# Turning the quantised x2 by DMA instead of by PE and VectorE

## The reference, cut to what matters

```
x = x + tanh(g_xattn) * attention(layernorm(x), ctx)      # 16 heads, int8-like quantised wq and wo
x = x + tanh(g_ffn)   * ffn(layernorm(x))

ffn(x): qx = fp8 values of x / scale, one scale per row
        g, u = qx @ qw_gate.T, qx @ qw_up.T, scaled       # 512 -> 1408
        t = silu(g) * u;  qt = fp8 values of t, one scale per row
        y = qt @ qw_down.T, scaled                        # 1408 -> 512
```

## Time and profile before

| | |
|---|---|
| median of 3 runs | 593.86 us (591.64, 595.87, 593.86) |
| span of the profiled execution, first to last instruction | 589.9 us |
| PE busy | 515.7 us (87%) |
| DVE busy | 516.0 us (87%) |
| ACT busy | 471.3 us (80%) |
| POOL busy | 227.2 us (39%) |
| one steady step, from x_in load to x_in load | 59.2 us |
| DMA, mean over the span | 49 GB/s |

### The profile page before, as it was taken

How to read it: one execution, slowest core, us unless ns; L and a number is a source line. 1 busy time by engine, 2 the same in 40 slices (tenths; PEclk the granted TensorE clock), 3 DMA queues, 4 the chain that set the end, 5 groups by cost and what they waited for, 6 DMA issues and landing times.

```text
span 589.9 us, 10832 instructions
## 1 busy us (share of the span) xinstructions
PE 515.7 (87%) x3456; PEld 326.7 (55%) x3456; DVE 516.0 (87%) x1294; ACT 471.3 (80%) x1148; POOL 227.2 (39%) x212
## 2 busy tenths in 40 slices
PE   0778689999999999999999999999999997965843
PEld 0665466567656765676567656765676554532311
DVE  4999989989799979997999799979997996599794
ACT  4499989999898989898989898989898987783251
POOL 4315134004632463246424642464245422452420
PEclk9899989999999999999999999999999998797888
DMA  8913233011002100210021001100100000000000
GB/s 265 386 62 98 99 108 104 6 54 38 1 2 84 44 0 2 79 47 3 1 74 54 1 1 59 68 2 2 54 37 1 1 2 37 0 2 0 36 1 36
DMA packets 14024, 28.75 MB, mean 49 GB/s; under 512 B 2576, under 2 KB 4624, under 8 KB 13968
## 3 DMA queue, kind: packets, MB, share of 16 engines
q1 hardware_dynamic: 9216, 16.65, 8.0%
q0 software_dynamic: 3328, 11.41, 5.7%
q10 hardware_dynamic: 1424, 0.01, 0.1%
HBM read 23.87 MB, written 4.19 MB: 48 GB/s over the span
## 4 chain that ended last, share of the span: by engine, by line
PE 52%; DVE 26%; issue 10%; ACT 2%; DVEq 0%; POOL 0%; POOLq 0%; ACTq 0%
PE bank_s L808 8%; PE bank_t L873 7%; PE bank_u L828 5%; PE bank_g L828 5%; PE bank_a L815 4%; PE bank_g L815 4%; DVE prob L1305 4%; PE bank_o L915 3%; DVE q L1200 3%; DVE t_sb L1195 2%; DVE t_sb L1239 2%; PE bank_a L839 2%; DVE ts L1490 2%; DVE v_sb L1229 1%; PE bank_g L1049 1%
## 5 line engine op out<-in xcount | busy, mean ns | idle before, releaser
L613 ACT ACTIVATE prob<-prob,neg_max 128x256 f32<-128x256 f32 x256 | 127.4, 505 | 2.5 <-DVE neg_max L1305 2.5
L1305 DVE CUSTOM_DVE_ANT_0 prob<-bank_s,mask_sb 128x256 f32<-128x256 f32 x256 | 96.3, 419 | 13.3 <-PE bank_t L873 5.0
L624 ACT ACTIVATE probT<-bank_t 128x512 f32<-128x512 f32 x128 | 74.0, 590 | 20.5 <-PE bank_t L873 17.2
L398 POOL TENSOR_TENSOR up<-up,wgu_scale 128x512 f32<-128x512 f32 (+1 forms) x42 | 54.9, 1306 | 89.1 <-ACT up L593 89.1
L873 PE MATMUL bank_t<-ident,prob 128*128 128x128 f32 x512 | 78.5, 281 | 3.6 <-ACT prob L613 2.4
L873 PEld LDWEIGHTS bank_t<-ident,prob 128*128 128x128 f32 x512 | 59.1, 143 | 30.3 <-issue 18.4
L808 PE MATMUL bank_s<-kf,qf 32*128 32x256 f32 x512 | 73.1, 403 | 1.9 <-DVE neg_max L1305 1.9
L808 PEld LDWEIGHTS bank_s<-kf,qf 32*128 32x128 f32 x512 | 44.0, 185 | 26.1 <-issue 19.6
L413 POOL TENSOR_TENSOR x<-x,y 128x512 f32<-128x512 f32 x14 | 19.6, 1400 | 96.9 <-DVE y L1503 96.9
L408 POOL TENSOR_TENSOR up<-gate,up 128x512 f32<-128x512 f32 (+1 forms) x42 | 54.4, 1296 | 4.2 <-DVE gate L1365 1.5
L613 ACT ACTIVATION_READ_ACCUMULATOR prob<-prob,neg_max 128x1 f32 x256 | 50.4, 197 | 0.0
(11 more groups left out here) (264 smaller groups left out, 1200.7 us busy)
## 6 DMA issues: line engine op xcount, KB each, us to landing
x_in<-in_x_dram SPq DMA_DIRECT2D x8, 512.0 KB
c_in<-in_ctx_dram SPq DMA_DIRECT2D x8, 512.0 KB
out_dram<-x POOLq DMA_DIRECT2D x7, 512.0 KB, 3.2
mask_sb<-in_mask_BxSxS_ff_dram SPq DMA_DIRECT2D x8, 256.0 KB, 3.7
t_sb<-in_L_ffn_w_down_dram SPq DMA_DIRECT2D x2, 704.0 KB, 5.5
t_sb<-in_L_ffn_w_down_dram POOLq DMA_DIRECT2D x2, 704.0 KB, 5.8
kf<-in_L_xattn_wq_dram SPq DMA_DIRECT2D x1, 1024.0 KB, 11.0
probT<-in_L_xattn_wk_dram SPq DMA_DIRECT2D x1, 1024.0 KB, 13.0
```

The lines of the kernel that those rows point to most:

```text
L398: pool.tensor_tensor(up[:, c % 2, 0:w], up[:, c % 2, 0:w], wu_scale[:, off:off + w], ALU.mult).then_inc(f["u_scaled"], 1)
L613: ins = act.activation(prob[:, head_par, t, :], prob[:, head_par, t, :], ACT.Exp, bias=neg_max[:, head_par, t:t + 1], scale=-1.0, accum_ou ...
L624: act.activation(probT[:, (slot + 3) % 4, :, :].rearrange("p a b -> p (a b)"), T_BANK[(slot + 1) % 2][:, :], ACT.Copy).then_inc(s["turned_ ...
L1305: ins = dve.tensor_tensor_reduce(prob[:, hp, t, :], S_BANK[hp][:, t * L:(t + 1) * L], mask_sb[:, hb, t, :], -1.0, 3.4e38, ALU.add, ALU.min ...
```

## The change

The eight PE transposes of `x2T_turn` and DVE's `x2T_copy` leave the orders of the steady steps and of the tail's batch k. In their place SP issues two DMA transposes per batch, each of one block t (128 x 512 bf16, 128 KB) from xq to its half of x2T. Each adds 16 to `x2T_ready`, so PE waits for 32 per batch. SP guards them: earlier products must have read x2T (`u_ps`, `g_ps`), and `q8_ready` must have reached block t. In a step they stand between the x_in load and the c_in load. Batch e of the tail keeps PE's transposes and DVE's copy.

```diff
@@ -291,14 +291,13 @@
             load8("q", wq)
 
             def step(b, par, A):
-                if not A:
-                    return
-
                 if not first_step(b):
                     need_alone(sp, (s["wq_loaded"], 16), (s["x_plus_ready"], b), (s["x_centred"], b))
                 else:
                     load8("k", wk)
                 sp.dma_start(x_in[:, :, :], x[bass.ds(b, 1)].rearrange("o (t p) c -> p (o t) c", p=P)).then_inc(s["x_loaded"], 16)
+                if b > 2:
+                    turn_x2(b - 1)
                 if not first_step(b):
                     need_alone(sp, (s["wq_loaded"], 16), (s["v_ps"], 2 * b))
                 sp.dma_start(c_in[:, :, :], ctx_in[bass.ds(b, 1)].rearrange("o (t p) c -> p (o t) c", p=P)).then_inc(s["ctx_loaded"], 16)
@@ -311,10 +310,21 @@
 
                 need_alone(sp, (s["wq_loaded"], 16), (s["masked"], 16 * (b - 1)))
                 sp.dma_start(mask_sb[:, par, :, :], mask[bass.ds(b, 1)].rearrange("o (t p) l -> p (o t) l", p=P)).then_inc(s[f"mask_loaded_{par}"], 16)
+            def turn_x2(b):
+
+                B2 = b - 2
+                for t in range(NT):
+                    need(sp, s["u_ps"], 1 + 6 * B2 if B2 else 0)
+                    need(sp, s["g_ps"], 6 * B2)
+                    sp.wait_ge(s["q8_ready"], JOBS * B2 + t + 1)
+                    sp.dma_start_transpose(x2T[:, :, t * P:(t + 1) * P], xq[:, t, :]).then_inc(s["x2T_ready"], 16)
+
             step(0, 0, True)
             step(1, 1, True)
             for b in range(2, NB):
                 step(b, b % 2, True)
+            for b in range(NB - 1, NB + 1):
+                turn_x2(b)
 
             sp.wait_ge(s["stored"], 16 * NB)
 
@@ -1022,7 +1032,7 @@
                 def up_project(slot):
                     c6 = slot - 5
                     if c6 == 0:
-                        pe.wait_ge(f["x2T_ready"], d - 1)
+                        pe.wait_ge(f["x2T_ready"], 32 * (d - 1) if f is s else 1)
                     pe.wait_ge(f["u_ready"], 1 + 6 * B2 + c6)
                     project_ffn(U_BANK, wuT, c6).then_inc(f["u_ps"], 1)
 
@@ -1086,7 +1096,7 @@
                 k.head_turn(0); k.ctxT_turn(0); k.oqT_turn(0); k.head_score(1); k.y_project(0); k.head_turn(1)
                 k.head_turn(2); k.ctxT_turn(1); k.group_pv(1); k.k_project_even(2); k.head_score(3); k.head_turn(3)
                 k.k_project_odd(2); k.head_turn(4); k.k_project_even(3); k.xT_turn(4); k.group_pv(5)
-                k.k_project_odd(3); k.xT_turn(5); k.head_turn(5); k.head_score(5); k.x2T_turn(5); k.sx_turn(6)
+                k.k_project_odd(3); k.xT_turn(5); k.head_turn(5); k.head_score(5); k.sx_turn(6)
                 k.head_turn(6); k.up_project(5); k.gate_project(5); k.q_project_0(6); k.up_project(6)
                 k.gate_project(6); k.head_turn(7); k.up_project(7); k.head_score(7); k.gate_project(7); k.head_turn(8)
                 k.up_project(8); k.q_project_1(7); k.gate_project(8); k.up_project(9); k.head_score(9); k.head_turn(9)
@@ -1099,7 +1109,7 @@
             def tail_order(k, e):
                 k.head_turn(0); k.oqT_turn(0); k.head_score(1); k.head_turn(1); k.group_pv(1); k.head_turn(2)
                 k.y_project(0); k.head_turn(3); k.head_score(3); k.head_turn(4); k.group_pv(5); k.head_turn(5)
-                k.head_turn(6); k.head_score(5); k.head_score(7); k.x2T_turn(5); k.head_turn(7); k.up_project(5)
+                k.head_turn(6); k.head_score(5); k.head_score(7); k.head_turn(7); k.up_project(5)
                 k.gate_project(5); k.up_project(6); k.head_turn(8); k.gate_project(6); k.up_project(7); k.group_pv(9)
                 k.head_turn(9); k.gate_project(7); k.head_turn(10); k.head_score(9); k.up_project(8)
                 k.gate_project(8); k.up_project(9); k.head_turn(11); k.head_turn(12); k.gate_project(9)
@@ -1534,7 +1544,7 @@
             def steady_step_order(k):
                 k.head_mask(0); k.head_mask(1); k.oqT_low(0); k.x_stats(0); k.y_scale(1); k.head_mask(2)
                 k.head_mask(3); k.x_scales(2); k.x2_stats(2); k.x2_centre(3); k.head_mask(4); k.x2_max(3)
-                k.head_mask(5); k.xT_low(5); k.x2_sum_0(4); k.x2_sub_0(4); k.x2_sum_1(4); k.x2_sub_1(4); k.x2T_copy(5)
+                k.head_mask(5); k.xT_low(5); k.x2_sum_0(4); k.x2_sub_0(4); k.x2_sum_1(4); k.x2_sub_1(4)
                 k.head_mask(6); k.sx_copy(7); k.head_mask(7); k.gate_scale(6); k.q_scale_0(7); k.gate_scale(7)
                 k.t_mul(7); k.head_mask(8); k.t_mul(8); k.gate_scale(8); k.head_mask(9); k.q_scale_1(8); k.t_mul(9)
                 k.gate_scale(9); k.t_scales(9); k.gate_scale(10); k.t_mul(10); k.head_mask(10); k.t_sum_0(10)
@@ -1547,7 +1557,7 @@
             def tail_order(k, e):
                 k.head_mask(0); k.head_mask(1); k.oqT_low(0); k.head_mask(2); k.head_mask(3); k.y_scale(1)
                 k.head_mask(4); k.head_mask(5); k.x2_stats(2); k.x2_centre(3); k.x2_max(3); k.head_mask(6)
-                k.head_mask(7); k.x2_sum_0(4); k.x2_sub_0(4); k.x2_sum_1(4); k.x2_sub_1(4); k.x2T_copy(5)
+                k.head_mask(7); k.x2_sum_0(4); k.x2_sub_0(4); k.x2_sum_1(4); k.x2_sub_1(4)
                 k.head_mask(8); k.gate_scale(6); k.head_mask(9); k.gate_scale(7); k.t_mul(7); k.t_mul(8)
                 k.gate_scale(8); k.head_mask(10); k.head_mask(11); k.gate_scale(9); k.t_mul(9); k.t_scales(9)
                 k.gate_scale(10); k.t_mul(10); k.o_norm(14); k.o_norm(15); k.gate_scale(11); k.o_max(15); k.o_max(14)
```

## The result

The changed kernel takes 602.4 us (median of 4 runs, 600.5 to 605.5) against 593.5 us before (4 runs): 8.9 us more, ratio 1.014, 95% interval 1.011 to 1.018. The profiled execution took 603.2 us with a span of 601.3, 11.4 us over the span of before. This one time also shows what lies around a span: 1.9 us. By that measure the 589.9 us of before belong to its fastest run, 591.64 us, and the 601.3 us to a run slightly above the median; so the profiles differ by more (11.4 us) than the medians (8.9 us).

A forecast was written before the change was run, and what follows sets the result against it. PE's order was taken as the path around the x2 turn. Six steps of 3.4 - 1.70 (10.2 us) plus 1.6 in the tail gave 11.8 us, on 593.86: 606 us, forecast range 600 to 614, wider range 595 to 630.

The forecast's parts named there:

- L: Time from the second q8_ready to the x2T_ready count of 32, ahead of the first up projection; taken as 3.4 us.
- the free 1.70 us: Time the DMA has after the second q8_ready in a step before PE would start later than today.
- The formula: Cost per batch at the first up projection is L - 1.70 us; 10.2 us for six steps.
- my lower bound of 2.2 from a plain copy: Low end for L: a plain copy of 128 KB, from the 512 KB store's 3.2 us less 0.96.
- 1.83 free: In the tail, from the second xq's end to the up projection: 1.83 us free, so 1.6 us of cost.
- a step of 60.9 us: Sign in the profile after: distance between x_in loads about 60.9 us against 59.2.
- 2 to 2.5 us of idle PE: Sign: PE idle ahead of the first up projection, released by a DMA into x2T, in each of seven places.
- rival A: Turned write costs nothing over a plain copy: L = 2.2, 3.4 us, 597 us (594 to 600), chance 0.25.
- The mask load: Nearest row for sizing L: 256 KB, queued right behind another transfer on SP, 3.7 us.
- rival C: PE's stall also lowers the clock, 1.7 us each, seven times: 618 us (614 to 630), chance 0.15.
- At most 0.40 to 0.55 us to gain: Largest gain per batch around the x2 turn: 0.55 us on PE, 0.40 us if DVE then holds.
- SP: SP's queue between the x_in and c_in loads: waits at q8_ready cost nothing, c_in about 33 us after x_in.

The follow-up runs named there:

- shadow: Kernel before, with PE's turn and DVE's copy kept, plus the same 14 DMA transposes from SP into space nobody reads: 593.8 us.
- split: Changed kernel with a semaphore per block of x2T, PE waiting for block 1 only ahead of the fourth up projection: 595.1 us.
- q first: Changed kernel with q_project_0 ahead of the first up projection on PE in the steady steps: 603.1 us.
- the third transpose: Changed kernel with an extra transpose of block 1 into unused space ahead of the second, PE waiting for all three: 615.4 us.
- tail by PE: Changed kernel with DMA transposes in the steps only; the tail's batch k is turned by PE and copied by DVE: 599.5 us.
- no turn: Only the first batch's x2 is turned and reused by the other six batches, PE waiting for their own xq alone: 595.0 us, repeated 594.6 us.

## Why the prediction was right, and where it was not

**The step's cost, L minus the free 1.70 us:** shown. The formula gave 0.82 from the measured L; the steps have 0.81. With the same transposes and no wait the cost is gone (shadow), with the wait moved nearly all of it is (split).

**The size of L:** the mis-sized term. I took 3.4 us, near the mask load; it is 2.5, close to my lower bound of 2.2 from a plain copy, so the term was 11.8 us and should have been 6 x 0.82 + 1.1 = 6.0 (the tail had L = 2.96 and 1.83 free). The consequences that I had named were too large with it: a step of 60.9 us (59.98 measured) and 2 to 2.5 us of idle PE (0.8 in five steps, 1.8 in one, 2.6 in the tail). With the measured L my own sum gives 593.86 + 6.0 = 600 us, the upper edge of rival A: a turned write at about the price of a plain copy was nearer to the truth than the forecast's L, and 2.52 lies only just above the 2.5 below which I had called the forecast wrong. The mask load was a poor neighbour: its 3.7 us begin while 512 KB ahead of it are still moving. The two transposes hardly touch, as their issues are 1.3 us apart and each moves for some 0.6 us.

**The rest, 2.9 of the 8.9 us:** two things that the sum left out. In the profile, whose difference is 11.4 us, they are the late landing (1.0 us more wait in one step of six), the clock behind it (1.7 us), and 3.2 us in the tail beyond its own wait. The clock is rival C, which I had counted as an alternative with its own 0.15; it came together with the short L, and in one of the six steps, not in each. I had no term for the late landing. How much of the tail's 3.2 us the transpose in it causes is not shown: with PE's turn back in the tail, 2.7 us of extra tail stayed in that profile. That the forecast of 606 was near 602.4 therefore owes something to luck: 5.8 us too much for L stand against 2.9 us that were missing.

**At most 0.40 to 0.55 us to gain:** wrong, 0.13. I looked at who would hold the path at its end (DVE, 0.40 idle at 341) and not at who is next at its start (ACT's exp, needed by head_turn(6)). A chain that names PE without a gap does not say how much later the next producer would have been.

**SP:** right. The c_in load goes out 33.9 us after x_in (33.1 before), late by nothing but the step's own growth of 0.8 us (usual step).

**What a transpose takes.** The Trainium skill's page "VectorE: DVE Perf Modes" ("The three transpose paths") gave 1309 ns per 128x128 block, 5.2 us for four in a row by my estimate; the transpose of four blocks landed in 2.5. The Trainium skill's page "Advanced Engine Details and Errata" ("X-Bar Transpose (TRN2)") has transposes as fast as regular DMAs. In bytes per second it is not so here: the view of the DMA engines, in 40 slices of 0.1 us from 329 us, shows two bursts of about 220 GB/s, while x_in moved at 377. (x_in comes from DRAM; no run has a plain copy inside SBUF.) For the time this mattered little: 128 KB take 0.60 us at 220 GB/s and 0.35 us at 377, so by this estimate 0.25 of the 2.5 us.

```profile
GB/s 20 20 41 20 0 0 0 0 0 0 0 0 74 212 225 220 212 215 123 29 0 0 0 0 0 41 184 225 223 220 207 166 42 3 0 0 0 0 0 0
```

**The late landing.** The two landings of one step took 4.0 us in the mean and 4.4 at most. It is no accident of one run: with q first they took 4.1 and 4.6 us in the same step, with the third transpose up to 3.6, while the other six kernels with transposes in that step have 3.2 at most, and all other steady steps have 2.3 to 2.6. Instructions are fetched in that step by DMA, 16 KB on queue 8, and the order in time differs. The two lines are GB/s in slices of 0.16 us, from 205.95 us in the changed kernel and from 210.50 with the tail by PE, both 3.2 us behind the x_in load:

```profile
GB/s 0 0 0 0 0 0 0 0 0 52 130 211 213 202 56 112 13 0 36 179 208 198 140 21 10 10 10 10 12 0 0 0 0 0 0 0 0 0 0 0
GB/s 0 0 0 0 0 0 0 0 0 52 101 211 216 206 80 8 10 0 21 166 221 203 193 28 0 0 0 0 0 0 0 0 0 104 0 0 0 0 0 0
```

In the first the fetch (the 112 between the two bursts, 208.4 us, 1.2 us long) comes before the second transpose's burst, whose last packets then trickle at 10 GB/s until 210.5. In the second it comes at 215.7 (the 104), behind all of them. In the three kernels with a landing of 3.6 us or more the fetch starts ahead of the last transpose's burst, in the six others behind the last packet. That fits a fetch in the way of some packets; no run moves the fetch alone, so it is not shown.

**Open.** How the lower clock in the tail answers to the start of the tail: split and no turn have steps 0.12 us shorter than before and no shorter time, and their tails differ by some 2 us in the profiles (101.3 and 99.0).

## What to carry to other kernels

A transfer that replaces engine work must be judged by when its data are first needed, not by what the engine sheds. Before pricing a removed instruction, look for the next producer that the same engine waits for: here it stood 0.13 us behind. If such a transfer is used all the same, give each piece its semaphore and wait where that piece is first read; that alone took back 7 of 9 us.

## What the runs showed of the hardware

A DMA transpose inside SBUF occupied SP for 1.2 us, and landed 2.3 to 2.6 us after its issue began, for 64 KB as for 128 KB, in all steady steps but the second, where it was 2.4 to 4.6. The data of 128 KB moved in 0.6 us of that, so several in a row are bound by their issue: four of 64 KB held SP for 5.0 us.

In the changed kernel an idle PE of 1.8 us, after 126 us at a granted clock of 1.00, was followed by 3.4 us at 0.50; after idle stretches of 0.8 us, in the other five steps, the clock stayed. Idle stretches of 2.1 us, in the kernel with the third transpose, had both outcomes: two falls in five.
